# Graph layer and routed experts: a table of rows written in pairs of tiles, with weight loads and clearings moved

## The chip, the cores and the metric

The kernel runs on one core of a Trainium2 chip. The metric is the device time of one execution in microseconds (us), the median of the runs shown. A difference of under 0.2% (2.6 us) is called no change here.

## What is computed

A graph layer over 1250 rows of 512 numbers, then a routed feed-forward stage with four experts, of which each row takes two. Cut to what matters:

```python
x = x + relu(batchnorm(aggr(xn) @ W_l.T + b_l + xn @ W_r.T))   # xn = layernorm(x); mean over 20000 edges
xf = layernorm(x)
topk_val, topk_idx = top_k(xf @ gate_w.T + gate_b, 2)
probs = softmax(topk_val)
for kk in range(2):
    for e in range(4):
        mask = topk_idx[:, kk] == e
        eo = expert_e(xf, mask)          # layernorm, attention over the rows of the mask, projection, MLP
        out += where(mask, eo * probs[:, kk], 0)
x = x + out
```

Each expert attends only among its own rows, in two groups (rows that have it as first choice and rows that have it as second), so the kernel first sorts the rows into lists.

## The kernel before

**The stages.** The graph layer takes about the first 360 us. It ends with `x2`, the 1250 rows as 10 tiles of 125 rows. Then comes the routing: DVE ranks the four gate values of each row, counts, and works out for each row its place in the list of its first and its second expert. Then four experts run one after the other, expert 0 with 4 tiles of 128 rows (128 rows in the first group, 384 in the second). Everything below happens between the graph layer and the middle of expert 0, from 360 to 450 us.

**Two ways into an expert.** All experts find their rows in `lists`, a DRAM array that 20 indirect DMAs (the scatters, L682, two for each tile of 125 rows) write from `rows`. For expert 0 there is a short cut, since it must start before the scatters are done: SP writes the normalised rows in their natural order into a DRAM array `table` (L524, one DMA for each tile, 125 rows of 2056 bytes), and POOL then gathers expert 0's first four tiles of 128 rows from there by number (L689).

**POOL's queue around the change, in program order.** First come the two scatters of tile 0 (L699), then a wait for all table writes (`s_lists`, L700) and for the row numbers (`s_index`, L701), then four gathers (L702). Three clearings follow (`total_rows`, `bias_rows`, `ones_k`, L703 to L705; each adds 1 to `s_econst`, which stands at 12 after them), the choice of the arm of the program that fits the expert's size, the other 18 scatters (L723), the copies of the values to `v_head` (L742), and a wait for all scatters (L765) before the copies for the second head of the first pair (L755 to L758), which PE's `turned_score(1, 0)` waits for.

**SP's queue, in program order.** The table writes, the marks (`marks_dram`, L526), a wait until those have landed, the choice of the arm, four pieces of expert 0's weights of 512 KB each (L541 and L488; pieces 6 to 9, which ACT rounds from 448 us on), the marks into `q_hi` and `k_hi` (L548), a wait for `s_econst` 12 (L554), the two bias rows into `den` (L556, 2 KB each), a wait for all scatters (L558), and then loads from `lists` and for expert 1.

**What waits for them.** ACT starts expert 0 with `first_rows(0)` and `first_rows(1)` (L993, L994): two tiles each, after gathers 0 and 1 (`s_ahead[0]`) and 2 and 3 (`s_ahead[1]`). PE turns these rows, ACT scales them, DVE splits them, and PE projects. DVE's `bias_halves` (L2208) splits the bias rows from `den` into `bias_rows` and sets `s_bias`. ACT waits for that (L1132) before the first exponential of the attention (L1095), and computes the first side of pair 1 (L1067) right behind the first two exponentials.

**How a DMA is cut.** The loads of `x` are written as 112 rows and 13 rows (`ROWS16 = 112`, L494); the writes to `out` (L513) and to `table` (L524) as 125 rows.

## Time and profile before

| | us |
|---|---|
| median of 3 runs | 1287.71 (1287.62 to 1289.76) |
| the profiled execution | 1292.2 |
| its span in the trace | 1290.4 |
| mean granted clock of TensorE | 0.906 |
| busy: PE, DVE, ACT, POOL | 1050.3, 731.5, 453.8, 329.3 |

The profiled execution is 4.5 us (0.35%) above the median, and 1.8 us of it lie outside the span. The page gives for each engine its busy time, then the span in 40 slices, the chain of work that ended last, and groups of instructions by line. In the slices of PE, most stand at 8 or 9 tenths; the twelfth and thirteenth (355 to 419 us) are the lowest after the first, with the clock at half.

```profile
PE   1986789998943887867886989989798899979984
...
PEclk9987799998655988989888989999999899989997
DMA  5192000000436424111323020000002112110010
```

In the rows of a timeline the first number is the start in us from the span's start and the second the time covered, from the first start to the last end; xN counts instructions. The idle time that the engine had before them, and what ended it, stands in brackets.

### The profile page before, as it was taken

What the parts mean: (1) busy time and instruction counts of PE and PEld (TensorE: products, weight loads), DVE (VectorE), ACT (ScalarE), POOL (GpSimd) and SP (SyncE); (2) the same over time, 40 slices, a digit from 0 to 9 for tenths busy, and PEclk for the clock granted to TensorE, in tenths of its full rate; (3) what the DMA queues carried; (4) which work ended last, traced back from release to release, by engine and by line L of the source; (5) the groups of instructions that cost most, each with busy time, mean ns of one, the idle gap of its engine ahead of it and who ended that gap; (6) DMA issues with size and microseconds to landing.
All of it is one profiled execution on the core that took longest, in us unless ns stands there. A gap on an engine that the chain in (4) does not pass through costs nothing.

```text
span 1290.4 us, 19562 instructions
## 1 busy us (share of the span) xinstructions
PE 1050.3 (81%) x5170; PEld 581.3 (45%) x5171; DVE 731.5 (57%) x1604; ACT 453.8 (35%) x843; POOL 329.3 (26%) x305
## 2 busy tenths in 40 slices
PE   1986789998943887867886989989798899979984
PEld 1654467777831343433443434434343335433332
DVE  5485635442371478636775565656748347745753
ACT  1301112221322465335626234434344442235521
POOL 3102233442745534214331030000000123203311
PEclk9987799998655988989888989999999899989997
DMA  5192000000436424111323020000002112110010
GB/s 152 46 276 88 2 2 0 0 0 1 145 104 192 130 66 164 44 66 49 115 88 123 1 66 1 1 0 0 0 0 82 50 39 71 56 58 1 1 32 34
DMA packets 36270, 75.63 MB, mean 59 GB/s; under 512 B 9644, under 2 KB 9942, under 8 KB 35915
## 3 DMA queue, kind: packets, MB, share of 16 engines
q1 hardware_dynamic: 27563, 55.91, 14.0%
q0 software_dynamic: 8320, 16.49, 4.4%
q10 hardware_dynamic: 288, 2.10, 0.5%
q8 instruction: 40, 0.66, 0.2%
q14 instruction: 59, 0.48, 0.1%
HBM read 49.06 MB, written 26.70 MB: 59 GB/s over the span
## 4 chain that ended last, share of the span: by engine, by line
PE 64%; DVE 14%; issue 9%; ACT 6%; DMA 3%; POOL 2%; SPq 1%; DVEq 1%; ACTq 0%; POOLq 0%
PE bank L1401 16%; PE bank L1492 9%; PE bank L1260 8%; PE bank L1299 5%; PE bank L1522 4%; PE bank L1577 3%; DVE den L2238 2%; PE bank L1295 2%; PE bank L1456 2%; PE bank L1477 2%; PE bank L1479 2%; PE bank L1226 2%; DMA table<-rows 1%; PE bank L1536 1%; PE bank L1561 1%
## 5 line engine op out<-in xcount | busy, mean ns | idle before, releaser
L1854 DVE TENSOR_SCALAR oh_src<-iota,edge 125x1250 f16 x178 | 101.5, 570 | 105.5 <-PE bank L1260 99.9
L1492 PE MATMUL bank<-probs_t,v_head 128*128 128x512 f32 (+1 forms) x288 | 147.0, 594 | 7.0 <-ACT probs_t L1044 6.4
L1044 ACT ACTIVATE probs_t<-bank 128x512 f32<-128x512 f32 x144 | 81.5, 573 | 135.9 <-PE bank L1479 135.3
L2151 DVE TENSOR_REDUCE mx<-bank 128x1 f32<-128x512 f32 x144 | 88.5, 657 | 63.8 <-PE bank L1456 62.9
L583 POOL TENSOR_TENSOR w<-w_stage,w 128x1024 f16<-128x1024 f32 x40 | 86.1, 2166 | 139.2 <-ACT w L852 139.2
L1260 PE MATMUL bank<-oh_src,oh_dst 125*125 x534 | 110.8, 357 | 2.8 <-issue 0.6
L1577 PE MATMUL bank<-probs_t,v_head 128*128 128x128 f32 (+2 forms) x192 | 88.7, 549 | 5.8 <-ACT probs_t L1095 4.3
L1401 PE MATMUL bank<-hT,w 128*128 128x256 f16 (+1 forms) x552 | 89.3, 325 | 1.4 <-DVE hT L2083 1.4
L1260 PEld LDWEIGHTS bank<-oh_src,oh_dst 125*125 x534 | 70.1, 142 | 43.7 <-issue 24.4
L1522 PE MATMUL bank<-hT,w 128*128 128x512 f16 x288 | 73.2, 387 | 7.8 <-ACT t L1069 7.8
L1401 PE MATMUL bank<-w,hT 128*128 128x512 f16 x264 | 67.5, 410 | 9.2 <-DVE hT L2083 9.2
L1401 PEld LDWEIGHTS bank<-hT,w 128*128 128x128 f16 (+1 forms) x552 | 56.8, 103 | 32.9 <-issue 2.8
L2224 DVE TENSOR_REDUCE mx<-bank 128x1 f32<-128x128 f32 (+2 forms) x96 | 48.9, 551 | 40.0 <-PE bank L1536 39.7
L1095 ACT ACTIVATE probs_t<-bank 128x128 f32<-128x128 f32 (+2 forms) x96 | 44.8, 488 | 72.9 <-PE bank L1563 72.3
L1492 PEld LDWEIGHTS bank<-probs_t,v_head 128*128 128x128 f32 x288 | 53.1, 195 | 29.5 <-ACT probs_t L1044 14.7
L1401 PE MATMUL bank<-w,oT 128*128 128x512 f16 x264 | 64.2, 395 | 0.0
L730 POOL COPY v_head<-x_in 128x640 f32 x6 | 4.3, 724 | 223.2 <-PE bank L1492 223.2
L956 ACT ACTIVATE t<-bank,ep 128x256 f32<-128x256 f32 x44 | 21.3, 564 | 109.4 <-PE bank L1702 109.4
L1456 PE MATMUL bank<-k_hi,q_hi 66*128 66x512 f16 x144 | 43.9, 382 | 18.8 <-DVE mx L2151 10.8
L1477 PE MATMUL bank<-q_hi,k_hi 97*128 97x512 f16 x144 | 54.8, 381 | 2.7 <-ACT q_hi L1022 2.7
L873 ACT COPY a_row<-bank 125x512 f32<-125x512 f32 (+1 forms) x30 | 13.3, 515 | 117.6 <-PE bank L1273 117.6
L1479 PE MATMUL bank<-q_both,k_both 128*128 128x512 f16 x144 | 54.4, 377 | 0.0
(316 smaller groups left out, 1951.0 us busy)
## 6 DMA issues: line engine op xcount, KB each, us to landing
w_stage<-in_ew_dram SPq DMA_DIRECT2D x40, 512.0 KB, 4.4
lists<-zeros SPq DMA_DIRECT2D x1, 10340.0 KB
x_in<-lists SPq DMA_DIRECT2D x15, 517.0 KB, 5.2
x_mem<-lists SPq DMA_DIRECT2D x3, 1024.0 KB, 5.2
x_mem<-lists SPq DMA_DIRECT2D x1, 2560.0 KB, 10.1
table<-rows SPq DMA_DIRECT2D x10, 251.0 KB
out_dram<-x_mem SPq DMA_DIRECT2D x10, 250.0 KB
big<-in_x_dram SPq DMA_DIRECT2D x10, 224.0 KB
```

Of the source, the lines that this page charges most:

```text
L583: nc.gpsimd.tensor_tensor(w16[:, 1, cols], w_stage[:, p % WB, :], w16[:, 0, cols], ALU.subtract).then_inc(s_elo, 1)
L1044: nc.scalar.activation(probs_t[:, x % NPB, 0:cn], stb[x % 2][:, 0:cn], ACT.Exp).then_inc(s_exp, 1)
L1260: last = nc.tensor.matmul(ab[k][0:TT, 0:cn], oh_dst[:, bass.ds(slot, 1), i, :], oh_src[:, bass.ds(slot, 1), i, c0:c0 + cn], start=False, s ...
L1401: last = nc.tensor.matmul(bank, lhs(a, c), rhs(b, c), start=(n == 0 and c == 0 and bias is None), stop=(n == 2 and c == chunks - 1))
L1456: nc.tensor.matmul(sbk[i % 2][:, 0:cn], q_hi[0:MARK + 2, hd, t * P:(t + 1) * P], k_hi[0:MARK + 2, hd, c0:c0 + cn], start=True, stop=True). ...
L1477: nc.tensor.matmul(stb[i % 2][:, 0:cn], k_hi[0:SHIFT + 1, hd, kt * P:(kt + 1) * P], q_hi[0:SHIFT + 1, hd, c0:c0 + cn], start=True, stop=False)
L1479: nc.tensor.matmul(stb[i % 2][:, 0:cn], k_both[:, hd, kt * P:(kt + 1) * P], q_both[:, hd, c0:c0 + cn], start=False, stop=True).then_inc(s_ ...
L1492: nc.tensor.matmul(pvb[(hd * nq + s) % 2][:, 0:cn], v_head[:, hd, kt, :], probs_t[:, (hd * nx + i) % NPB, 0:cn], start=(k == 0), stop=(k = ...
L1522: last = nc.tensor.matmul(pp[0][:, 0:nt * P], w16[:, a, c0:c0 + P], hT[b][:, c, 0:nt * P], start=k == 0, stop=k == 3 * KC - 1)
L1577: nc.tensor.matmul(pvb[(hd * nq + s) % 2][:, 0:cn], v_head[:, hd, j % 2 * nt + kt, :], probs_t[:, i, 0:cn], start=(k == 0), stop=(k == nk ...
L1854: nc.vector.tensor_scalar(oh_src[:, bass.ds(slot, 1), i, 0:N].rearrange("p a n -> p (a n)"), iota[:, :], edge[:, 0, i, bass.ds(g, 1)], Non ...
L2151: nc.vector.tensor_reduce(mx[:, hd, t, s:s + 1], sbk[i % 2][:, 0:cn], AX.X, ALU.max).then_inc(s_mx, 1)
```

## The change

The change has four parts. The table is written in five pairs of tiles, each pair as one DMA of 112 rows of each tile and one of the other 13 rows. SP waits for gathers 2 and 3 (`s_ahead[1]`) before the later weight pieces of an expert. The three clearings on POOL go from between the gathers and the scatters to behind the scatters. ACT runs one more activation (`Identity` on one number for each row, result never read) after the exponential of the routing.

```diff
@@ SP @@
-            for t in range(NT):
-                sp.wait_ge(s_xf, t + 1)
-                sp.dma_start(table[1 + t * TT:1 + (t + 1) * TT, :], rows[:, t, 0:D + 2]).then_inc(s_lists, 16)
+            table_t = table[1:N + 1, :].rearrange("(t p) d -> p t d", p=TT)
+            for b in range(NB):
+                sp.wait_ge(s_xf, 2 * b + 2)
+                for r in (slice(0, ROWS16), slice(ROWS16, TT)):
+                    sp.dma_start(table_t[r, 2 * b:2 * b + 2, :],
+                                 rows[r, 2 * b:2 * b + 2, 0:D + 2]).then_inc(s_lists, 16)
...
             def expert_sp(e, shape):
                 nt = shape.nt
+                sp.wait_ge(s_ahead[1], 32)
                 for p in range(QKV_P, NWP):
                     load_piece(e, p)
@@ POOL @@
             gather(range(AHEAD))
-            nc.gpsimd.memset(total_rows[:, 0:2, :], 0.0).then_inc(s_econst, 1)
-            nc.gpsimd.memset(bias_rows[:, :], 0.0).then_inc(s_econst, 1)
-            nc.gpsimd.memset(ones_k[:, :], 1.0).then_inc(s_econst, 1)
             pool.wait_ge(s_arms, 1)
...
                     scatter(range(SPARE // 2, NT))
+                    nc.gpsimd.memset(total_rows[:, 0:2, :], 0.0).then_inc(s_econst, 1)
+                    nc.gpsimd.memset(bias_rows[:, :], 0.0).then_inc(s_econst, 1)
+                    nc.gpsimd.memset(ones_k[:, :], 1.0).then_inc(s_econst, 1)
                 copied.skip(nt)
@@ ACT @@
             nc.scalar.activation(gap[:, 1, :], gap[:, 0, :], ACT.Exp).then_inc(s_ex, 1)
+            nc.scalar.activation(unread[:, :], rrstd[:, 0:1], ACT.Identity, scale=1.0)
```

The order of instructions on three engines shows what moved. On POOL, at the end of the routing and the start of expert 0, the order before is (`total_rows`, `bias_rows` and `ones_k` are the clearings, the DMA to `lists` a scatter, the one from `table` a gather):

```order
62 L682 DMA lists<-rows,slots 5120x517 x2
63 L689 DMA x_in<-table,first_rows_i 128x514 x4
64 L703 MEMSET total_rows 128x1024
65 L704 MEMSET bias_rows 128x1024
66 L705 MEMSET ones_k 128x128
67 L127 ISA
68 L128 TENSOR_LOAD arms
69 L128 ISA x2
70 L130 COMPARE_AND_BRANCH x4
71 L132 UNCONDITIONAL_BRANCH
72 L719 COMPARE_AND_BRANCH
73 L682 DMA lists<-rows,slots 5120x517 x18
```

and the order of the changed kernel at the same place is:

```order
62 L687 DMA lists<-rows,slots 5120x517 x2
63 L694 DMA x_in<-table,first_rows_i 128x514 x4
64 L127 ISA
65 L128 TENSOR_LOAD arms
66 L128 ISA x2
67 L130 COMPARE_AND_BRANCH x4
68 L132 UNCONDITIONAL_BRANCH
69 L721 COMPARE_AND_BRANCH
70 L687 DMA lists<-rows,slots 5120x517 x18
71 L726 MEMSET total_rows 128x1024
72 L727 MEMSET bias_rows 128x1024
73 L728 MEMSET ones_k 128x128
```

The clearings stand behind the last of 18 scatters now; the two scatters of tile 0 and the four gathers stay where they were.

On ACT, from the rows of the table to the first instruction of expert 0, the order before is (`gap` is the exponential of the routing, `probs_t` the first rows of the expert):

```order
74 L929 ACTIVATE rows<-x_mem,row_shift,rrstd 125x512 x10
75 L932 ACTIVATE gap<-gap 125x10
76 L127 ISA
77 L128 TENSOR_LOAD arms
78 L128 ISA x2
79 L130 COMPARE_AND_BRANCH x4
80 L132 UNCONDITIONAL_BRANCH
81 L137 ISA
82 L992 REGISTER_ALU
83 L982 REGISTER_ALU
84 L984 ACT_TABLE_LOAD
85 L984 ACTIVATE probs_t<-x_in 128x512 x4
```

and of the changed kernel:

```order
75 L937 ACTIVATE gap<-gap 125x10
76 L938 ACTIVATE unread<-rrstd 125x1
77 L127 ISA
78 L128 TENSOR_LOAD arms
79 L128 ISA x2
80 L130 COMPARE_AND_BRANCH x4
81 L132 UNCONDITIONAL_BRANCH
82 L137 ISA
83 L998 REGISTER_ALU
84 L988 REGISTER_ALU
85 L990 ACT_TABLE_LOAD
86 L990 ACTIVATE probs_t<-x_in 128x512 x4
```

The activation on `unread` has come in, and no load of a function table stands before it; the load at the first activation of the arm is there as before.

## Rows read from the trace of the kernel before

**Rows 1.** The chain of waits, 355 to 420: start us, us, what
```profile
364.23 7.17 ACT rows L929 x10
...
377.74 17.79 DMA table<-rows
...
400.35 7.81 DMA x_in<-table,first_rows_i
```

**Rows 2.** Busy time of each engine, clock and DMA in four stretches
```profile
core 0: us, PE busy (x) PEld busy (x) DVE busy (x) ACT busy (x) POOL busy (x), PEclk, DMA share, GB/s
372.00:378.00 6.00, 2.37 (x35) 1.64 (x36) 5.59 (x31) 0.00 (x0) 0.00 (x0) 0.50 0.33 116
12.00:19.00 7.00, 0.90 (x4) 0.17 (x2) 5.28 (x18) 0.00 (x0) 0.34 (x1) 1.00 0.96 238
402.00:408.00 6.00, 1.97 (x8) 1.57 (x8) 0.00 (x0) 2.62 (x3) 5.00 (x6) 0.50 0.99 358
414.00:430.00 16.00, 13.74 (x58) 5.63 (x56) 6.55 (x14) 4.13 (x7) 12.82 (x11) 0.92 0.68 172
```

**Rows 3.** POOL in order of time: start us, us, line, out<-in, idle before
```profile
379.68 3.75 POOL L682 DMA_INDIRECT lists<-rows,slots  x1 [13.19 <-DMA table<-rows]
383.74 1.21 POOL L682 DMA_INDIRECT lists<-rows,slots  x1 [0.30 <-issue]
396.35 1.06 POOL L689 DMA_INDIRECT x_in<-table,first_rows_i  x1 [11.40 <-DMA table<-rows]
...
400.35 1.00 POOL L689 DMA_INDIRECT x_in<-table,first_rows_i  x1 [0.30 <-issue]
401.33 0.98 POOL L703 MEMSET total_rows<- 128x1024 f32 x1
...
403.56 1.24 POOL L682 DMA_INDIRECT lists<-rows,slots  x1 [0.22 <-issue]
...
429.52 1.19 POOL L682 DMA_INDIRECT lists<-rows,slots  x1 [0.31 <-issue]
...
438.62 0.61 POOL L755 COPY q_both<-halves 64x512 f16<-64x512 f16 x1 [2.64 <-DMA lists<-rows,slots]
```

**Rows 4.** DMA issues of SP in order of time
```profile
366.56 13.13 SPq L524 DMA_DIRECT2D table<-rows  x10
384.34 0.41 SPq L526 DMA_DIRECT2D marks_dram<-marks  x1
398.44 2.60 SPq L488 DMA_DIRECT2D w_stage<-in_ew_dram  x4
...
403.55 0.66 SPq L556 DMA_DIRECT2D den<-in_erow_dram  x2
```

**Rows 5.** ACT in order of time, 355 to 475 us
```profile
402.88 1.28 ACT L984 ACT_TABLE_LOAD   x1 [31.39 <-DMA x_in<-table,first_rows_i]
...
408.57 1.33 ACT L984 ACTIVATE probs_t<-x_in 128x512 f32<-128x512 f32 x2 [3.06 <-DMA x_in<-table,first_rows_i]
...
435.73 0.82 ACT L1095 ACTIVATE probs_t<-bank 128x128 f32<-128x128 f32 x2 [0.53 <-PE bank L1563]
438.65 0.69 ACT L1067 ACTIVATE halves<-bank,ep 128x512 f16<-128x512 f32 x1 [2.10 <-PE bank L1522]
```

**Rows 6.** DVE in order of time, 355 to 475 us
```profile
378.33 0.16 DVE L2010 CAST first_rows_i<-bank 128x4 int32<-128x4 f32 x1
...
433.10 0.42 DVE L2213 CAST bias_rows<-den 1x512 f16<-1x512 f32 x1
...
434.69 0.68 DVE L2214 TENSOR_TENSOR bias_rows<-den,bias_rows 1x512 f16<-1x512 f32 x1
```

**Rows 7.** PE in order of time: expert 0, second head
```profile
448.37 0.23 PE L1561 MATMUL bank<-q_hi,k_hi 97*128 97x128 f16 x1 [0.46 <-ACT q_hi L1075]
```

**Rows 8.** DMA issues by line, in two stretches: size, us to landing
```profile
marks_dram<-marks SPq DMA_DIRECT2D x1, 40.0 KB, 12.6
...
x_in<-lists SPq DMA_DIRECT2D x1, 15.0 KB, 2.5
```

More of the change, by code:

```diff
@@ L178, in program @@
         arms = sb("arms", [1, NE], I32)
+        unread = sb("unread", [TT, 1], F32)
         slots = sb("slots", [TT, NT, 2], I32)
```

## The prediction, made before the changed kernel was run

> **What bounds the kernel now.** I read the slices of the page first: PE is busy 8 or 9 tenths of nearly every slice, but hardly at all from about 364 to 405 us, between the graph layer and expert 0. The change touches only that stretch and the start of expert 0, so the rest of the kernel matters only as something that is moved as a whole. Next I read the chain of waits through the stretch [rows 1]. Three steps make it up. ACT writes the normalised rows from 364.23 to 371.40. The table writes land at 377.74 + 17.79 = 395.53. The gathers follow, and the last of them lands at 400.35 + 7.81 = 408.16. DVE, which works out the lists, is done long before: the row numbers for the gathers are ready at 378.33 + 0.16 = 378.5 [rows 6]. So from 378.5 to 395.5 nothing is waited for but the table.
>
> Why the table takes so long stands in the busy times by stretch [rows 2]. From 372 to 378 us only table writes are under way, and the DMA share is 0.33 at 116 GB/s, with 0.33 x 16 = 5.3 engines' worth of work. From 12 to 19 us the load of x, which is cut into 112 and 13 rows, runs at 0.96 and 238 GB/s, although its last part thins out. With weights and gathers together (402 to 408) it is 0.99 and 358 GB/s. The table has 1250 x 2056 bytes = 2.57 MB; at 116 GB/s that is 22 us, and with the start-up it gives the 29 us from the first issue at 366.56 [rows 4] to 395.53.
>
> **Part 1, the table in pairs.** At 238 GB/s the 2.57 MB take 10.8 us, at 358 GB/s 7.2 us. The first pair can go at 366.56 as now. The last pair is ready when ACT is, at 371.4. So the table lands between 371.4 + 2.5 (what a small transfer takes from issue to landing [rows 8]) = 373.9 and 366.6 + 10.8 + 2.5 = 379.9. I need not choose, because POOL isn't there yet: it waits for the slots and the row numbers until 378.5, then runs the first two scatters, of which the first takes 3.75 us and the second ends at 383.74 + 1.21 = 384.95 [rows 3]. Even the slow end is covered by 5 us; only below 2.57 MB / 16 us = 160 GB/s would the table be last again. The first gather then starts at 384.95 + 0.3 = 385.25 instead of 396.35: **11.1 us earlier**. The 3.75 us are the one odd piece in this. Other scatters take 1.2, so if the traffic of the table made this one slow, up to 2.5 us more are to be had; if it is the price of a first indirect DMA, nothing. The first gather shows no such start, which leaves both open, and I take nothing.
>
> The rule behind the 0.33 is in the Trainium skill, page DMA: Bandwidth & Descriptors, section Why a DMA increments its semaphore by 16 and not by 1: a DMA runs on the largest number of engines up to 16 that divides its slowest dimension, so 125 rows get 5, 112 get 16, and 13 get 13. The trace agrees, with its 5.3 of 16. The same page, section Rules for kernel authors, speaks against the cut ("Two transfers to disjoint partition halves: Don't bother — they serialize") and would leave the table where it is; that is the first rival below.
>
> **Part 2, the weights wait for the gathers.** Gather 1 ends on POOL at about 398.7 (four gathers, 1.33 apart, from 396.35), and ACT starts at 402.88 [rows 3, 5]: 4.2 us. Gather 3 ends at 401.35, and ACT starts on it at 408.57: 7.2 us. Between them lie 4 x 512 KB of weights, issued from 398.44 to 401.04 [rows 4], which fill the DMA engines to 0.99 [rows 2]. Without them I take 4.2 us for gather 3 also, with 7.2 as the other bound (scatters follow the gathers more closely now, and the two first scatters run just ahead of them). POOL ends gather 3 at 401.35 - 11.1 = 390.25, so the rows are there at 394.45. ACT is free by then: gathers 0 and 1 come at 402.88 - 11.1 = 391.8, the table load of 1.28 and two activations of 1.33 end at 394.4. So `first_rows(1)` starts at 394.45 instead of 408.57: **14.1 us earlier**, 11.1 at the other bound. What is late for it: the weight pieces issue at about 394.5 to 397.1 and land some 6 us later; ACT rounds them only behind the exponentials of the first head, which begin at 435.73 now [rows 5]. The marks in `q_hi` and `k_hi`, queued behind them on SP, are needed for expert 0's first scores, which come shortly before DVE's bias rows at 433.10 [rows 6], over 20 us behind `first_rows(1)` at 408.57. Both are covered. In the later experts the wait has long been met and costs nothing.
>
> SP must be past the marks DMA for this. It is issued at 384.34 [rows 4] and took 12.6 us to land [rows 8], behind the table on the same queue. With the table gone I expect 3 to 5 us, so SP is at its new wait by about 391, before the gathers land.
>
> **Part 3, the clearings behind the scatters.** They take from 401.33 to 403.34 (403.56 less the idle 0.22), 2.0 us [rows 3], and the scatters begin that much earlier. The 18 scatters take from 403.56 to 430.71 = 27.15 us. Now they start at 390.25 + 0.3 = 390.55 and end at 417.7; the clearings end at 419.7. This turns a wait that cost nothing into one that counts. SP issues the bias rows after the clearings: 0.2 us later, the second of the two at 420.25, landed by 422.75 with 2.5 us as for the small load [rows 4, 8]. DVE splits them in 435.37 - 433.10 = 2.27 us [rows 6], to 425.0. Before the exponentials ACT waits for exactly this. They stand at 435.73 now and would come at 435.73 - 14.1 = 421.6; they come at 425.1 and end at 425.95. Of these 3.5 us ACT has 2.1 us of slack, its idle time before L1067 at 438.65 [rows 5]. L1067 now starts at 425.95, and 438.65 - 425.95 = 12.7. So of the 14.1 us **1.4 are given back**. Since the bias rows hang on POOL's queue and not on the gathers' landing, the result is the smaller of two: the gathers' gain (11.1 to 14.1) and this 12.7.
>
> Also behind POOL's queue are the copies for the second head. The last scatter ended at 430.71 and the first copy started at 438.62, 7.9 us later; now that is 417.7 + 7.9 = 425.6, and with four copies of 0.61 us and a little between them they are done at about 428.4. PE wants them at 448.37 [rows 7] - 12.7 = 435.7. This is covered by 7 us. Loads from `lists` on SP follow the same landing and keep their distance.
>
> **Part 4, the activation on `unread`.** The order of the changed kernel shows no load of a function table in front of it and still shows the one at the first activation of the arm, which lies behind the wait for the gathers. So the 1.28 us [rows 5] stay on the path. The added activation runs at 371.5 in idle time: nothing. If the load were gone, ACT would be ready at 393.1, but gather 3 lands at 394.45 anyway. The Trainium skill, page ScalarE activation tables: per-element evaluation and per-set limits, section Table sets in the compiler and the runtime, says that loads are placed block by block; the order of both kernels agrees.
>
> **The sum.** 11.1 (table) + 3.0 (weights) - 1.4 (bias rows) = 12.7 us. The profiled execution goes from 1292.2 to 1279.5, and the median, 4.5 us below it, from 1287.71 to **1275.0**. PE's clock changes little in this: it is granted 0.50 (1.2 GHz) through the stretch and 0.92 from 414 to 430 [rows 2], and it will rise behind the first products as before. Where it rises and falls later can shift by some us of the time, which I put at 1.5 us either way.
>
> **The rivals.** (a) *The cut doesn't help*, because the two transfers serialize on the same engines. Then gathers stay at 396.35 and only parts 2 and 3 act: the clearings end at 430.8, the bias rows land at 433.9, L1067 starts at 437.05 instead of 438.65. That is 1.6 us, 1286.1. Against it speaks the 238 GB/s of the load cut in this way. 4 in 100. (b) *Less is given back or more gained*: the first scatter takes 1.2 instead of 3.75 us, or the bias rows land in under 1.5 us. Then 14 to 16 us, 1272 to 1273.7; 14 in 100. (c) *The gathers or scatters are slowed by each other*: gathers land after 7.2 us, or the scatters take 1.7 us each. Then 9 to 11 us, 1276.7 to 1278.7; 14 in 100. (d) *Slower than before*: POOL's scatters become the bound through the bias rows. The clearings must end later than 419.7 + 12.7 = 432.4, so each of the 18 scatters must take 1.5 + 0.7 = 2.2 us; at 2.5 us the kernel would stand at 1275.0 + 18 x 1.0 = 1293. Now they overlap the weights, and a scatter's descriptors could be held up by full queues. But three scatters ran beside the weights before, in the stretch with a share of 0.99, 1.5 us apart. 3 in 100.
>
> **How the numbers follow.** The forecast of 12.7, with 11.2 to 14.2 around it, has 65 in 100. The range takes in (b) and most of (c), and reaches from 1287.71 - 16 = 1271.7 to 1278.7. Faster by over 0.2% (under 1285.1) are all but (a) and (d): 0.93; within 0.2% 0.04; slower 0.03.
>
> **What would show it.** The table lands by 380. The first gather starts near 385.3, `first_rows(1)` near 394.5, the last scatter ends near 417.7. DVE's L2213 waits 3 to 4 us for a DMA before it, and the exponentials follow at once. The table load of 1.28 us is still there at about 391.8. From L1067 on, everything stands 12.7 us earlier and keeps its distances. I am wrong if a DMA share of about 0.33 remains from 367 to 378, if the scatters come further apart than 1.5 us, or if the distance of the two kernels changes by more than 2 us after 450.

## The result, and the profile of the changed kernel

The changed kernel takes 1284.6 us, the median of 20 executions (1276.65 to 1292.78). The kernel before, run beside it, has 1289.22 us (20 executions, 1286.76 to 1294.26). The ratio is 0.995, with a 95% interval of 0.9933 to 0.9967. By this ratio it is 0.5% faster, half of the 1.0% that was forecast, and 1284.6 lies outside the range of 1271.7 to 1278.7.

The profiled execution took 1278.63 us with a span of 1276.7 us and a granted clock of 0.915. That is 13.6 us under the profiled execution of before, close to the forecast of 12.7. It is one of the quick executions of its kernel, 6 us below the median. Whoever compares these two profiles alone finds the forecast confirmed, and that is luck: of the span's 13.7 us, 10.6 arise between ACT's first row and the attention of expert 0, 1.1 lie ahead of that row, and the rest lies behind, in work that was not changed. Other executions of the same kernel show what the forecast missed.

The stretch of the table writes, busy times, clock and DMA share (it answers to the first line of [rows 2]):

```profile
core 0: us, PE busy (x) PEld busy (x) DVE busy (x) ACT busy (x) POOL busy (x), PEclk, DMA share, GB/s
366.00:372.00 6.00, 0.14 (x2) 0.00 (x0) 5.31 (x43) 4.51 (x9) 0.00 (x0) 0.50 0.90 275
372.00:378.00 6.00, 2.95 (x42) 2.05 (x42) 5.69 (x29) 0.00 (x0) 0.00 (x0) 0.50 0.48 158
```

While ACT still writes rows, the DMA engines are at 0.90 and 275 GB/s. The 0.48 behind it is a mean over a stretch in which the writes end: the last of them have landed by 376 us. POOL and SP in order of time (as in [rows 3, 4]; idle time before and its releaser in brackets):

```profile
378.57 3.76 POOL L687 DMA_INDIRECT lists<-rows,slots  x1 [13.15 <-issue]
...
384.14 1.06 POOL L694 DMA_INDIRECT x_in<-table,first_rows_i  x1 [0.30 <-issue]
...
416.10 0.97 POOL L726 MEMSET total_rows<- 128x1024 f32 x1
```

```profile
365.49 7.60 SPq L527 DMA_DIRECT2D table<-rows  x10
383.22 0.41 SPq L530 DMA_DIRECT2D marks_dram<-marks  x1
396.10 5.51 SPq L489 DMA_DIRECT2D w_stage<-in_ew_dram  x4
...
418.31 0.65 SPq L561 DMA_DIRECT2D den<-in_erow_dram  x2
```

The first gather no longer waits for the table. It starts 12.2 us earlier than in [rows 3], of which 1.1 us belong to what lies ahead (ACT's first row is at 363.16 instead of 364.23): 11.1 us, the forecast to the tenth. Then ACT, as in [rows 5]:

```profile
363.16 7.16 ACT L934 ACTIVATE rows<-x_mem,row_shift,rrstd 125x512 f32<-125x512 f32 x10 [7.46 <-DVE row_shift L1927]
...
394.24 1.28 ACT L990 ACT_TABLE_LOAD   x1 [23.73 <-DMA x_in<-table,first_rows_i]
395.53 2.56 ACT L990 ACTIVATE probs_t<-x_in 128x512 f32<-128x512 f32 x4
...
426.47 0.66 ACT L1101 ACTIVATE probs_t<-bank 128x128 f32<-128x128 f32 x2 [3.79 <-DVE bias_rows L2220]
427.03 0.68 ACT L1073 ACTIVATE halves<-bank,ep 128x512 f16<-128x512 f32 x1
```

There is no second wait as the one before 408.57 in [rows 5]: while ACT loads its table and takes the first two tiles, the other two land. The profile gives for each gather the time from issue to landing (9.0, 8.6, 7.7 and 7.3 us), which puts the landings at 393.1, 394.1, 394.5 and 395.4. The table of functions is still loaded. L1073 (L1067 of before) starts 11.6 us earlier than in [rows 5], 10.6 if both are counted from ACT's first row. That start is the mark by which the runs below are compared.

### The profile page after: what moved, and what is told of

The parts are those of the page before. It is cut to its first block, busy times and chain, and to the rows that moved or that the text cites. A ratio compares the mean times of both kernels' runs of the same rounds, so it can differ in the third digit from the quotient of the medians.

```text
span 1276.7 us, 19567 instructions
## 1 busy us (share of the span) xinstructions
PE 1046.0 (82%) x5170; PEld 579.7 (45%) x5171; DVE 731.6 (57%) x1604; ACT 453.5 (36%) x844; POOL 328.5 (26%) x305
## 4 chain that ended last, share of the span: by engine, by line
PE 63%; DVE 16%; issue 10%; ACT 4%; POOL 3%; DMA 1%; DVEq 1%; SPq 0%; ACTq 0%; POOLq 0%
PE bank L1407 16%; PE bank L1498 9%; PE bank L1266 8%; PE bank L1305 5%; PE bank L1528 3%; PE bank L1583 3%; DVE den L2244 3%; PE bank L1462 2%; PE bank L1301 2%; PE bank L1483 2%; PE bank L1485 2%; PE bank L1232 2%; POOL lists L687 2%; DVE oT L2246 1%; PE bank L1542 1%
## 5 line engine op out<-in xcount | busy, mean ns | idle before, releaser
L1407 PE MATMUL bank<-hT,w 128*128 128x256 f16 (+1 forms) x552 | 89.6, 326 | 1.6 <-DVE hT L2089 1.6
L1407 PE MATMUL bank<-w,hT 128*128 128x512 f16 x264 | 66.0, 403 | 9.6 <-DVE hT L2089 9.6
L1407 PEld LDWEIGHTS bank<-hT,w 128*128 128x128 f16 (+1 forms) x552 | 57.0, 103 | 33.3 <-issue 3.0
L1498 PEld LDWEIGHTS bank<-probs_t,v_head 128*128 128x128 f32 x288 | 53.0, 195 | 29.1 <-ACT probs_t L1050 14.7
L1407 PE MATMUL bank<-w,oT 128*128 128x512 f16 x264 | 64.2, 396 | 0.0
L1462 PE MATMUL bank<-k_hi,q_hi 66*128 66x512 f16 x144 | 43.1, 375 | 16.0 <-DVE mx L2157 10.6
L878 ACT COPY a_row<-bank 125x512 f32<-125x512 f32 (+1 forms) x30 | 13.3, 515 | 119.1 <-PE bank L1279 119.1
```

The source lines that it names most:

```text
L1407: last = nc.tensor.matmul(bank, lhs(a, c), rhs(b, c), start=(n == 0 and c == 0 and bias is None), stop=(n == 2 and c == chunks - 1))
L1462: nc.tensor.matmul(sbk[i % 2][:, 0:cn], q_hi[0:MARK + 2, hd, t * P:(t + 1) * P], k_hi[0:MARK + 2, hd, c0:c0 + cn], start=True, stop=True). ...
L1498: nc.tensor.matmul(pvb[(hd * nq + s) % 2][:, 0:cn], v_head[:, hd, kt, :], probs_t[:, (hd * nx + i) % NPB, 0:cn], start=(k == 0), stop=(k = ...
```

## The experiments

"Mark" is the start of L1073 (first side of pair 1), and "load" that of the table of functions, both in us after ACT's first row, from each kernel's profile. For before the mark is 438.65 - 364.23 = 74.4.

| kernel | median us (runs) | ratio to before, 95% | load | mark |
|---|---|---|---|---|
| changed | 1284.6 (20) | 0.995 (0.9933 to 0.9967) | 31.1 | 63.9 |
| a_again, the same | 1283.69 (12) | 0.9953 (0.9931 to 0.9976) | 32.7 | 67.9 |
| a_third, the same | 1282.18 (12) | 0.994 (0.9921 to 0.996) | 30.9 | 68.0 |
| a_fourth, the same | 1283.72 (12) | 0.9961 (0.9941 to 0.998) | 30.6 | 66.8 |
| no_wait | 1283.73 (12) | 0.9955 (0.9934 to 0.9976) | 30.9 | 67.9 |
| no_table | 1290.96 (12) | 1.0013 (0.9999 to 1.0027) | 37.2 | 76.3 |
| table_only | 1278.84 (8) | 0.9927 (0.9897 to 0.9957) | 31.3 | 63.7 |
| no_clear | 1279.96 (7) | 0.9936 (0.9911 to 0.996) | 30.7 | 63.6 |
| clear_dve | 1281.55 (6) | 0.9937 (0.9925 to 0.995) | 30.5 | 63.1 |
| clear_dve_again | 1278.17 (6) | 0.9925 (0.9901 to 0.9949) | 30.4 | 61.5 |
| dummy_clear | 1280.94 (5) | 0.9934 (0.9921 to 0.9946) | 30.2 | 63.5 |
| dve_dummy | 1281.46 (6) | 0.9928 (0.9904 to 0.9951) | 30.6 | 67.9 |
| long_dummy | 1283.88 (12) | 0.9951 (0.9927 to 0.9975) | 30.7 | 63.4 |
| port_long | 1288.28 (12) | 0.9989 (0.9975 to 1.0004) | 30.7 | 68.2 |
| gather_first | 1276.38 (6) | 0.9908 (0.9891 to 0.9926) | 23.1 | 57.6 |
| best | 1278.76 (6) | 0.9916 (0.9893 to 0.9939) | 23.3 | 58.0 |
| marks_later | 1294.27 (10) | 1.0039 (1.0023 to 1.0055) | 27.1 | 80.5 |

Executions of one kernel spread over some 10 us, so single medians of 5 or 6 runs say little below 2 us. Three things move the time without any of the edits. ACT's first row starts at 362.5 to 366.0 us. The time from the mark to the last activation lies between 828.5 and 834.2 us over these profiles for the same work; it is shortest in the first profile of the changed kernel, and what moves it was not followed. And PE's clock rises early in some executions: from 400 to 404 us it is granted 0.90 in the first profile of the changed kernel, where the first twelve matmuls of L1407 take 2.76 us, 0.81 in clear_dve_again (3.24 us), and 0.50 in table_only, no_clear and clear_dve (4.45 to 4.89 us). That is why clear_dve_again has its mark 1.7 us ahead of clear_dve.

**The table alone, and all but the table.** table_only is the kernel before with this edit, and no_table the changed kernel with it taken back:

```
-            for t in range(NT):
-                sp.wait_ge(s_xf, t + 1)
-                sp.dma_start(table[1 + t * TT:1 + (t + 1) * TT, :], rows[:, t, 0:D + 2])...
+            for b in range(NB):
+                sp.wait_ge(s_xf, 2 * b + 2)
+                for r in (slice(0, ROWS16), slice(ROWS16, TT)):
+                    sp.dma_start(table_t[r, 2 * b:2 * b + 2, :], rows[r, 2 * b:2 * b + 2, 0:D + 2])...
```

> The kernel before with the table in pairs alone; clearings and weights as before. T1 and T2: the table lands before 380 and the first gather starts near 384 (11 to 12 us earlier). T1: gathers 2 and 3 land behind the weights, as in before 7 us after POOL ends them, and the exponentials are not held by the bias rows: 9 to 11 us faster than before in most runs, narrow spread. T2: 3 to 6 us faster with the rest given back behind 450 us.

> The changed kernel with the table written in ten DMAs of 125 rows as before: parts 2 to 4 alone. My prediction's sum for this was 1.6 us faster than before. If the weights' wait gives nothing, and the clearings cost 3 to 5 us when they meet DVE's copies, it is 0 to 5 us slower than before. In before the weights did land ahead of gathers 2 and 3, so here the wait should bring first_rows(1) about 2.5 us forward.

table_only has 1278.84 us, a ratio of 0.9927: by its median the table alone gains more than the whole change, though the intervals overlap. no_table is 1.0013, so everything else gains nothing, and if anything loses. Its DVE and ACT show where the time stays:

```profile
436.81 0.42 DVE L2216 CAST bias_rows<-den 1x512 f16<-1x512 f32 x1 [9.90 <-DMA den<-in_erow_dram]
```

```profile
401.11 1.28 ACT L987 ACT_TABLE_LOAD   x1 [29.80 <-DMA x_in<-table,first_rows_i]
...
439.67 0.66 ACT L1098 ACTIVATE probs_t<-bank 128x128 f32<-128x128 f32 x2 [10.98 <-DVE bias_rows L2217]
```

Here the wait for the gathers does work. SP issues the weights at 404.41, behind the gathers' landing, and gathers 2 and 3 come with the first two: `first_rows(1)` starts 4.5 us earlier than in before, from ACT's first row. But POOL's scatters end as late as before, the clearings behind them at 430.1, and the bias rows are issued from 430.30 on and are there 5.4 us after the second issue is over. ACT waits 10.98 us for them, and the mark is 1.9 us later than in before. That is the wait which the forecast named in part 3, grown to where it eats the gain of part 2.

**The weights' wait.** no_wait is the changed kernel without this line:

```
-                sp.wait_ge(s_ahead[1], 32)
```

> The changed kernel without SP's wait for gathers 2 and 3 before the weights. If the weights slow the gathers, first_rows(1) starts 2 to 3 us later and the time is 1 to 3 us longer than the changed kernel's; if the gathers land late for the two scatters ahead of them (in the first profile all four landed at about 394 to 396, 7 us after POOL), it changes by less than 1 us.

> The changed kernel once more, nothing altered, for a second profile. Over 20 runs it is 0.5% faster, spread over 16 us, and its first profiled execution is one of its fast ones (1278.6). Theory T1: the gain of the stage from 360 to 430 us varies from run to run, because the gathers and the two bias rows land behind scatters and weights; then an execution near the median shows the first activation of expert 0 or the exponentials later than 394 and 426 us by as much as it is slower, up to 8 us. Theory T2: the stage always gains about 10.5 us against the end of the graph layer, and 3 to 8 us are given back in the experts behind 450 us; then the stage looks as in the first profile and the later distances are longer.

1283.73 against 1283.69 us for the changed kernel beside it: no gain shows, with intervals of 2.8 us to either side. SP in both, first no_wait, then a_again:

```profile
386.04 0.41 SPq L530 DMA_DIRECT2D marks_dram<-marks  x1
397.47 3.69 SPq L489 DMA_DIRECT2D w_stage<-in_ew_dram  x4
```

```profile
383.53 0.41 SPq L530 DMA_DIRECT2D marks_dram<-marks  x1
397.63 4.15 SPq L489 DMA_DIRECT2D w_stage<-in_ew_dram  x4
```

SP is held by the landing of the marks in both, which takes 9.1 us in the changed kernel, 9.4 in no_wait and 9.0 in table_only. The forecast had 3 to 5 us. Without the new line the weights go out 1.4 to 2.0 us behind that landing (table_only, no_wait), when gathers 0 and 1 are there or nearly so. With it SP waits some 2 us more. What SP waited for in the first profile of the changed kernel (total us, times, longest):

```profile
SPq L122 <- DMA marks_dram<-marks: 8.6, 1, 8.6
SPq L488 <- DMA x_in<-table,first_rows_i: 1.8, 1, 1.8
```

In a_again the second wait is 3.0 us, in a_fourth 1.5. So the new line is met late, but it holds nothing back that could hurt: gather 3 lands at 395.4 in the changed kernel, and ACT, busy with its table and the first two tiles until 396.8, would have stood a later landing. The 2 us go to what is queued behind the weights, the marks' lists for PE (below).

**The scatters ahead of the gathers.** gather_first has the clearings in their old place, and all 20 scatters behind the gathers; best has the clearings on DVE instead:

```
-            scatter(range(SPARE // 2))
...
-                    scatter(range(SPARE // 2, NT))
+                    scatter(range(0, NT))
```

> As no_clear, but all 20 scatters go behind the gathers, so the gathers start at 378.6 instead of 384.1 and nothing is queued ahead of them. Theory Q: the gathers land 7 us after POOL has made them because the two scatters of tile 0 (and the marks) are ahead; then they land 4 us after it, the first activation of expert 0 starts 6 to 8 us earlier than in no_clear, and the time is 1272 to 1275. Theory R: a landing of 7 us belongs to the gathers themselves; then the first activation starts 1.5 to 3.5 us earlier (the first indirect DMA takes 3.8 us wherever it stands), and the time is 1276 to 1279.

> All 20 scatters behind the four gathers, and the three clearings on VectorE behind the copy for the expert's first norm. If the order on POOL's queue is what held the gathers and the clearings what held the copies: 1274 to 1277 us (gather_first had 1276.4 with the clearings in front of the scatters; here POOL has 2.2 us less ahead of the first scatter), marks landing within 7 us, the table of functions loaded at 23 us after ACT's first row. If the clearings are in the way on VectorE: no better than 1279 us.

gather_first, POOL and ACT:

```profile
379.56 3.68 POOL L694 DMA_INDIRECT x_in<-table,first_rows_i  x1 [13.00 <-issue]
383.55 1.02 POOL L694 DMA_INDIRECT x_in<-table,first_rows_i  x1 [0.31 <-issue]
```

```profile
387.43 1.28 ACT L989 ACT_TABLE_LOAD   x1 [15.77 <-DMA x_in<-table,first_rows_i]
388.72 1.33 ACT L989 ACTIVATE probs_t<-x_in 128x512 f32<-128x512 f32 x2
392.72 1.33 ACT L989 ACTIVATE probs_t<-x_in 128x512 f32<-128x512 f32 x2 [2.67 <-DMA x_in<-table,first_rows_i]
```

Gather 1 is there 387.43 - 384.57 = 2.9 us after its end on POOL, as ACT sees it. In the changed kernel it ends at 386.52 and ACT starts at 394.24, 7.7 us later. This looks like the work of the scatters ahead. But gather 3, which ends at 387.17 here and has no scatter ahead either, is there only at 392.72, 5.6 us later (the last gather of the changed kernel, by its landing at 395.4: 6.3). What lies between gathers 1 and 3 here is the marks' transfer, issued at 384.60.

Both kernels have lower medians than the changed one, 1276.38 and 1278.76 us; from table_only (1278.84) and from each other they are not told apart. best was expected at 1274 to 1277 us and misses that: its table is loaded at 23 us and its marks land in 6.2 us as expected, but PE waits 1.23 us for a list whose issue stands behind 6.46 us of weight issues (3.75 in gather_first). The odd 3.7 us are settled: whichever indirect DMA comes first takes them, here a gather.

**The marks behind the gathers.** marks_later is clear_dve, with its two scatters ahead of the gathers, and on SP:

```
             sp.wait_ge(s_marks, 1)
+            sp.wait_ge(s_ahead[1], 32)
             sp.dma_start(marks_dram.rearrange("e s g (p i) -> p (e s g) i", i=PER),
```

> clear_dve with the marks' transfer on SP behind the landing of the four gathers; the two scatters of tile 0 still run ahead of the gathers. If the marks' small pieces are what the gathers land behind: ACT loads its table 2.5 to 4.5 us after gather 1's end on POOL instead of 7.1 to 7.7, and first_rows(1) starts 3 us earlier (about 30 us after ACT's first row instead of 33); the marks themselves land in under 7 us. If it is the scatters ahead: ACT starts about 7 us after gather 1 as in clear_dve. The median says little: weights and lists are issued later (at about 399 instead of 395 us), so PE may wait for a list and give the gain back; 1276 to 1284 us.

POOL, ACT, SP and PE:

```profile
387.45 1.01 POOL L695 DMA_INDIRECT x_in<-table,first_rows_i  x1 [0.30 <-issue]
```

```profile
392.17 1.28 ACT L988 ACT_TABLE_LOAD   x1 [19.73 <-DMA x_in<-table,first_rows_i]
```

```profile
393.88 0.41 SPq L531 DMA_DIRECT2D marks_dram<-marks  x1
408.19 5.59 SPq L489 DMA_DIRECT2D w_stage<-in_ew_dram  x4
```

```profile
430.45 4.78 PE L1405 MATMUL bank<-w,hT 128*128 128x512 f16 x12 [19.15 <-DMA k_hi<-marks_dram]
```

This tells them apart. With the scatters ahead but the marks away, gather 1 is there 392.17 - 388.46 = 3.7 us after its end, and `first_rows(1)` starts 3.4 us earlier than in clear_dve (29.6 instead of 33.0 after ACT's first row). The gathers land late behind the marks' transfer. Issue plus time to landing, for the marks and for gathers 0 to 3:

| kernel | marks land | gathers land | us after their end on POOL |
|---|---|---|---|
| changed | 392.3 | 393.1, 394.1, 394.5, 395.4 | 7.9, 7.6, 6.7, 6.3 |
| no_table | 396.7 | 399.4, 400.9, 402.4, 403.8 | 2.2, 2.5, 2.6, 2.7 |
| gather_first | 391.1 | 385.6, 387.2, 391.8, 392.7 | 2.3, 2.7, 5.9, 5.5 |
| marks_later | 405.5 | 390.9, 392.1, 392.8, 393.8 | 3.7, 3.6, 3.0, 2.7 |

The first gather issued behind the marks lands within a microsecond of them (392.3 and 393.1, 391.1 and 391.8), and so it is in every other profile with the marks ahead. The two scatters ahead cost at most about 1 us (3.7 against 2.3 us for gather 0). The weights cost nothing here, since they go out too late. The rest of the expectation failed by far: the marks now go out among 18 scatters and take 11.6 us, SP reaches the weights at 408.19, and PE waits 19.15 us for its list. By its ratio the kernel is 5 us slower than before. The marks have to be early; they can't simply be moved.

**The clearings.** no_clear is the changed kernel with the three clearings back in front of the scatters. clear_dve has them on DVE, behind the copy for expert 0's first norm:

```
-                    nc.gpsimd.memset(total_rows[:, 0:2, :], 0.0).then_inc(s_econst, 1)
-                    nc.gpsimd.memset(bias_rows[:, :], 0.0).then_inc(s_econst, 1)
-                    nc.gpsimd.memset(ones_k[:, :], 1.0).then_inc(s_econst, 1)
...
+            nc.vector.memset(total_rows[:, 0:2, :], 0.0).then_inc(s_econst, 1)
+            nc.vector.memset(bias_rows[:, :], 0.0).then_inc(s_econst, 1)
+            nc.vector.memset(ones_k[:, :], 1.0).then_inc(s_econst, 1)
```

> The changed kernel with the three clearings back in front of the 18 scatters, so that the bias rows load early. In the first profile of the changed kernel the exponentials waited 3.8 us for the bias rows and L1073 (the first side of pair 1) started 1.1 us late for it. T1: this wait is gone, the runs are 1 to 4 us faster than the changed kernel and spread less. T2: within 1.5 us of the changed kernel, with the same spread.

> The changed kernel with the three clearings on DVE, which is idle from about 384 to 399 us, instead of POOL. Both theories: no slow DVE copy, bias rows early; POOL's scatters start right behind the gathers. 1278 to 1280, 4 to 6 us under the changed kernel, and at most 1 us from no_clear.

> The changed kernel with its clearings on VectorE, once more, beside a_fourth and port_long. Both theories: no copy of 64x512 above 0.5 us, first side of pair 1 at 63 to 64 us after ACT's first row, median 1280 to 1282 us.

The four runs without late POOL writes (table_only, no_clear, clear_dve twice) have a mean ratio of 0.9931, the four of the changed kernel 0.9951. The clearings behind the scatters cost about 0.2%, 2.6 us; over all executions but one of 1298.4 us, 27 against 55, the means are 1280.0 and 1283.5 us. Why shows in the second and third profiles of the changed kernel. a_again, DVE, POOL and PE:

```profile
415.82 2.08 DVE L2203 COPY k_hi<-halves 64x512 f16<-64x512 f16 x1
417.91 0.29 DVE L2204 COPY k_both<-halves 64x512 f16<-64x512 f16 x1
```

```profile
415.75 0.97 POOL L726 MEMSET total_rows<- 128x1024 f32 x1
416.64 0.97 POOL L727 MEMSET bias_rows<- 128x1024 f16 x1
417.53 0.22 POOL L728 MEMSET ones_k<- 128x128 f16 x1
```

```profile
418.63 0.54 PE L1542 MATMUL bank<-k_hi,q_hi 66*128 66x128 f16 x2 [2.24 <-DVE k_both L2206]
418.97 4.39 PE L1407 MATMUL bank<-w,hT 128*128 128x512 f16 x12
```

> The changed kernel once more, for how often POOL's clearings and VectorE's copies meet. If they meet in the profile: a copy of 64x512 of 2 to 3 us, the first side of pair 1 at 67 to 68 us after ACT's first row. If they do not: 63 to 65 us. The median in either case 1282 to 1286 us.

> The changed kernel once more. If the stall of VectorE's copy is what costs most of the time: it is there in this profile too with 3 chances in 4 (first side of pair 1 at 67 to 68 us after ACT's first row, else 63 to 65), and the median stands 2 to 4 us above that of clear_dve_again, which runs beside it. If not, no more than 1 us.

A copy of 64x512 that takes 0.28 us in the first profile takes 2.08 us and ends 0.15 us after the last memset. In a_third it is the next copy, 3.00 us, again ending 0.15 us behind the memsets; in no_wait the one after that, 3.00 us. In a_third and no_wait the record of the held copy begins 0.8 us before the first memset, while POOL still issues the last scatter. PE waits for it, and its granted clock falls: 0.73 from 419 to 425 us in a_again and a_third against 1.00 in the first profile, where twelve matmuls of L1407 take 2.76 us instead of 4.39. What this costs shows from DVE's subtraction in front of these copies (L2202 and its like) to the mark: 12.3 to 12.6 us in table_only, no_clear, clear_dve and clear_dve_again, 15.7 in a_again, 16.5 in a_third and 16.7 in no_wait, so 3.4 to 4.4 us more than in clear_dve. The rest of a_again's late mark is older: its table of functions is loaded 1.6 us later than in the first profile. There the copies start 1.65 us ahead of the clearings (414.45 and 416.10) and pass. That is why it looked undisturbed.

a_fourth has its mark late too (15.9 us over the same stretch), but for another reason. Its copies are short, and PE waits for a list:

```profile
416.38 4.45 PE L1407 MATMUL bank<-w,hT 128*128 128x512 f16 x12 [2.46 <-DMA k_hi<-marks_dram]
```

SP issues `q_hi` and `k_hi` behind the four weight pieces. Those issues take 6.58 us in a_fourth and 8.51 in dve_dummy, where PE waits 5.43 us for the same list; in clear_dve and clear_dve_again they take 3.98 and 3.77. Why the issues take longer in one execution than in another is open. The new wait of SP for the gathers adds 1.5 us to the lateness in a_fourth. The expectation for a_fourth, a held copy with 3 chances in 4, did not come out; its median lies 5.6 us above clear_dve_again, where 2 to 4 were expected.

**POOL writes without the clearings' job.** Four kernels keep the bias rows early and let POOL write unused parts of `x_in`. dummy_clear (on no_clear) and dve_dummy (on clear_dve) have memsets of the clearings' sizes behind the scatters, long_dummy two copies of 125x1024 there. port_long is clear_dve with:

```
-                    scatter(range(SPARE // 2, NT))
+                    scatter(range(SPARE // 2, NT - 1))
+                    nc.gpsimd.tensor_tensor(x_in[0:TT, 4:6, 0:D], rows[:, 0:2, 0:D], rows[:, 2:4, 0:D], ALU.subtract)
+                    nc.gpsimd.tensor_tensor(x_in[0:TT, 6:8, 0:D], rows[:, 0:2, 0:D], rows[:, 2:4, 0:D], ALU.subtract)
+                    scatter(range(NT - 1, NT))
```

> The kernel with the clearings in front of the scatters (as in no_clear, 1280.0), plus three clearings of unused parts of x_in, of the same sizes, behind the 18 scatters. The bias rows load early, so they can't hold the exponentials. Theory P (port): in two profiles of three with the clearings behind the scatters, a DVE copy of 64x512 fp16 took 2.08 and 3.00 us instead of 0.28 and ended 0.1 us after POOL's clearings; PE then idled 2.2 us, and its clock stood at half for the next 3.4 us. Then these clearings do the same: median 1283 to 1285, 3 to 5 us above no_clear. Theory B (bias rows): the 4 us between no_clear and the changed kernel are the wait for the bias rows; then this stays at 1279 to 1281.

> The changed kernel with its three real clearings on VectorE (as in clear_dve, so that the bias rows' transfers start early) and three memsets of unused parts of x_in (1024, 1024 and 128 columns) on POOL behind the 18 scatters, so that POOL writes at the time at which it does in the changed kernel, and nothing waits for it. If it is POOL's writing that costs (VectorE's copies of 64x512 stand still beside it, and TensorE's clock falls behind them): 1283 to 1285 us, one copy of L2203 to L2212 takes 2 to 3 us instead of 0.28, and the first side of pair 1 starts 67 to 68 us after ACT's first row. If it is the bias rows' wait that costs: 1280 to 1282 us as clear_dve, the first side at 63 to 64 us. If the memsets fall between the copies, the profile shows no long copy, and the median alone says how often they meet.

> As dve_dummy, but instead of the memsets two POOL copies of 125x1024 from the normalised rows into unused parts of x_in, which nothing waits for (2.3 us each, worked out from L744's 0.6 us for 256 columns). They run from 415.6 to about 420.2, past the time of VectorE's copies at 419.6 to 420.1 in clear_dve. If POOL's work beside VectorE's copies holds these: a copy of 64x512 that takes 1 to 3 us and ends with a POOL copy, the median at 1283 to 1286 us. If it does not: copies of 0.28 us, and 1281 to 1282 us.

> clear_dve with two POOL subtractions of 125x1024 (about 2.2 us each by L588) from the normalised rows into unused parts of x_in, ahead of the last tile's two scatters: they run from about 50.2 to 54.6 us after ACT's first row, over the time at which VectorE copies the first half's sides of k (51.3 to 53.7 in the profiles so far). Nothing waits for them; the last scatters come 4.4 us later. If VectorE's copies stand still beside POOL's work: a copy of 64x512 that takes 1 to 3.5 us and ends with a subtraction, TensorE's clock at half behind it, the first side of pair 1 at 66.5 to 68.5 us after ACT's first row, and the median at 1284 to 1286 us. If late clearings cost through the bias rows alone: copies of 0.28 us, the first side at 63 to 64 us, and 1280.5 to 1282 us.

The first three decide little. The medians of dummy_clear and dve_dummy lie where they were expected if the bias rows alone cost, that of long_dummy where it was expected if POOL's work does. But in their profiles POOL's writes fell behind the copies (in long_dummy 417.87, with the last copy over at 417.1), so no copy was held; the late mark of dve_dummy is the list named above. The medians are 1280.94, 1281.46 and 1283.88, and why long_dummy stands higher its profile, with the mark at 63.4, does not say. port_long covers the copies' time by design. POOL, then DVE:

```profile
415.90 2.01 POOL L726 TENSOR_TENSOR x_in<-rows 125x1024 f32<-125x1024 f32 x1
417.85 2.00 POOL L727 TENSOR_TENSOR x_in<-rows 125x1024 f32<-125x1024 f32 x1
```

```profile
416.63 3.78 DVE L2205 TENSOR_TENSOR halves<-t,halves 128x512 f16<-128x512 f32 x1 [2.81 <-ACT t L1075]
420.33 0.28 DVE L2206 COPY k_hi<-halves 64x512 f16<-64x512 f16 x1
```

The bias rows are issued at 407.81 here, far ahead of need, and nothing waits for the subtractions. Yet DVE's subtraction takes 3.78 us instead of 0.69 and ends 0.6 us after POOL's second one, PE waits 3.92 us, its clock is granted 0.72 from 421 to 427, and the mark is at 68.2. The median is 1288.28 us, 10.1 above clear_dve_again beside it. That is more than the 1284 to 1286 expected, and more than the stretch shows: the mark is 6.7 us later, 1.8 of them ahead of the subtraction, where PE's first twelve matmuls ran at the lower clock (4.83 instead of 3.24 us), and 4.9 from it on (17.2 us to the mark instead of 12.3). The last scatters also come 4 us later in this kernel, and that part was not taken apart. That POOL's work holds DVE, and that this costs 3.4 to 4.9 us up to the mark, is shown; how much of a median it makes is not. The held instruction here is a subtraction, though, and not a copy as expected.

The Trainium skill, page SBUF — State Buffer, section Who interferes with whom, has the rule: VectorE and GpSimd share a pair of ports, a copy in a two-port mode competes for it, an operation with two inputs in SBUF does so with a GpSimd instruction that reads SBUF, and "the other fully blocks". The traces agree for the copy beside memsets (2.08 instead of 0.28 us) and for the subtraction beside a reading POOL (3.78 instead of 0.69 us). The page has the lock last one instruction; in a_again the copy waited through all three memsets, and in a_third and no_wait through the end of a scatter's issue as well.

## Why the prediction was wrong, step by step

**What bounds, and the table: right.** The first gather came 11.1 us earlier, as worked out. From that alone the forecast had 11.1 us; table_only measured a ratio of 0.9927, 9.4 us (5.5 to 13.3 by its interval), and 10.8 us in the mark. The cut runs at a DMA share of 0.90 instead of 0.33, so rival (a) is out. The rule of the Trainium skill that the forecast cited against the cut (page DMA: Bandwidth & Descriptors, section Rules for kernel authors) gives as its reason that both halves already use all 16 engines; the table's 125 rows, with a share of 0.33, did not, and the run shows the gain that the rule taken by its words denies.

**Part 2, "Without them I take 4.2 us for gather 3 also": wrong, 3.0 us.** For the traffic of before the mechanism was right: in no_table, with the weights held back, the gathers land 2.2 to 2.7 us after their end on POOL, and `first_rows(1)` starts 4.5 us earlier than in before. The 4.2 us for gather 1 even had some weights in them already, issued from 398.44 on. What failed is that this landing was carried over to the kernel with the early table, for gather 3 and for gathers 0 and 1 ("come at 402.88 - 11.1 = 391.8"). There the gathers follow the marks' transfer by 0.9 us instead of 12 and land behind it: gather 1 7.6 us after its end, gather 3 6.3 us after. So ACT's table load starts at 31.1 us after its first row, 7.6 us earlier than in before and not 11.1. From there ACT's own work sets `first_rows(1)`, 10.7 us earlier and not 14.1; without the marks ahead it is 14.7 (marks_later). The prediction had the other bound, 7.2 us and a gain of 11.1, but gave it the scatters as the reason and chose the other end. The weights' term itself measures as nothing once the table is early (no_wait against a_again).

The other leg failed with it: "with the table gone I expect 3 to 5 us" for the marks. They took 9.1. The slow table was some 3.5 us of the 12.6 in [rows 8] (12.7 in no_table, 8.4 to 9.4 in the kernels with the table in pairs and two scatters ahead). The rest goes with POOL's DMAs about it: 6.5 us with fewer of them under way in gather_first, 11.6 among the scatters in marks_later. And "both are covered" does not hold for the lists in `q_hi` and `k_hi`. The forecast placed their use shortly before 433.10, but PE's first scores with them (L1536) start at 427.96 in before and at 415.45 in the changed kernel; in a_fourth PE waits 2.46 us for them.

**Part 3, the bias rows: the mechanism right, the size off both ways.** The wait came, 3.46 us on DVE and 3.79 on ACT. The landing took 5.3 us where the forecast took 2.5 from a 15 KB load in another place of the program. It cost 0.9 us, against 1.4 forecast: from PE's score matmul at 422.81 (L1567), in front of the first exponential, to the mark it is 4.22 us, and 3.32 in table_only, no_clear, clear_dve and a_again. The gathers had come late too, which made room for it, and where a copy was held it cost nothing. In no_table, where the gathers came later still but the clearings did too, the same wait costs 1.9 us more than before. There rival (a) had 1.6 us gained; most of the difference is the landing, put at 2.5 us.

**What was not there at all: who shares a port with the moved work.** The three clearings were costed by their length and by who waits for them. Where they were before, DVE was idle (0.00 from 402 to 408 in [rows 2]). Behind the scatters they meet the copies of expert 0's second product, on which PE waits at once. Three profiles show the collision (a_again, a_third, no_wait) of five with the late clearings, no_table aside. It costs 3.4 to 4.4 us when it comes. These three, the 0.9 us of the first profile and nothing in a_fourth, where PE waited for the list, have a mean of 2.6 us, an estimate that fits the 2.6 us by ratios. PE's slower matmuls are 1.6 us of it (4.39 instead of 2.76 us), the size that the forecast allowed for shifts of the clock. The timeline of before has these copies on DVE:

```profile
426.57 0.28 DVE L2197 COPY k_hi<-halves 64x512 f16<-64x512 f16 x1
426.86 0.29 DVE L2198 COPY k_both<-halves 64x512 f16<-64x512 f16 x1
427.16 0.67 DVE L2200 COPY k_both<-halves 64x512 f16<-64x512 f16 x1
```

The third takes 0.67 instead of 0.28 us and ends 0.1 us after a scatter's issue (426.08 + 1.63 on POOL), so the hold was there to be seen in a small form. Moved by the 14.1 us that part 2 had for the gathers' side they would be done by 413.7, 4 us ahead of the clearings, which the forecast put at 417.7 to 419.7. Moved by the 10.7 us that came they end at 417.1, within 1 us of them. So the error of part 2 hid this one, and a look at the copies by its own numbers would have found 4 us of room; by the other bound, 11.1, it would have been 1 us.

**Part 4: right.** The load of 1.28 us is still there.

**The sum.** By ratios the forecast was 1275.0 / 1287.71 = 0.9901 and the result 0.995, a miss of 6.3 us. By the runs 3.0 are the weights' term, 1.7 the table's (11.1 forecast, 9.4 in table_only), and 1.2 the clearings' (1.4 forecast, 2.6 from the mean ratios above), which leaves 0.4. This split is an estimate: each measured term has an interval of 2 us or more, and the 1.7 of the table is not told apart from nothing (its mark has 10.8). The weights' term rests on the profiles, in which `first_rows(1)` comes 3.4 us later than forecast. The rest of the distance in microseconds comes from the base: before had 1289.22 us in the comparison, 1.5 over the median that the forecast started from, and ratio and medians differ by some tenths of a per cent themselves. Rival (c) named "gathers land after 7.2 us" and gave it 1276.7 to 1278.7; it was the case that came, though behind the marks and not behind scatters, and with less left than it had, since it knew nothing of the held copies.

## What to carry to other kernels

Before moving cheap work on POOL out of an idle stretch, look at what DVE does where it lands: a memset of 1 us that nobody waits for can hold a copy that PE waits for, and PE's clock falls with it. When a change makes a transfer earlier, look for the transfer that it runs into there, one of many small pieces above all, and take its landing time from one of the same kind in the same traffic. A profile is one execution: where the spread is 10 us, take the kernel's profile more than once before believing a stretch.

## What the chip showed that was not expected

- Small transfers land late in this stretch: 40 KB of marks after 9.1 us (12.6 before, 6.5 in gather_first, 11.6 in marks_later), 2 KB of bias rows after 5.3 us. Gathers issued behind the marks land only after them, 3 to 4 us later than without (7.6 and 6.3 us after POOL's end against 3.6 and 2.7 in marks_later).
- A DVE copy of 64x512 can be held by POOL's memsets until 0.15 us after the last of them (2.08 and 3.00 us instead of 0.28), and for some tenths of a us by a scatter's issue (0.67 us in before).
- The first indirect DMA of the kernel takes 3.7 us on POOL whether it scatters (3.76) or gathers (3.68); most of the others take 1.0 to 1.25.
- Four weight issues of the same sizes keep SP's queue for 2.42 us (no_clear) to 8.51 us (dve_dummy), and the lists behind them can come 5.43 us too late for PE.
